# The second attention of a two-layer kernel: stages ordered engine by engine, router logits in groups of four tiles

## The reference

```python
h = _layernorm(x, axis=-1) * (1 + ca) + sa
x = x + ga * _L1_attn_ref(h, L1_attn_Wq, L1_attn_Wk, L1_attn_Wv, L1_attn_Wfc)
h = _layernorm(x, axis=-1) * (1 + cb) + sb
x = x + gb * _L1_ffn_ref(h, L1_ffn_Wg, L1_ffn_W1, L1_ffn_W2)
```

```python
Q = (x @ Wq.T).reshape(b, s, h, hd)
K = (x @ Wk.T).reshape(b, s, h, hd)
V = (x @ Wv.T).reshape(b, s, h, hd)
scores = jnp.einsum('bshd,bstd->bsht', Q, K) / math.sqrt(hd)
attn = jax.nn.softmax(scores, axis=-1)
out = jnp.einsum('bsht,bstd->bshd', attn, V).reshape(b, s, dm)
return out @ Wfc.T
```

## Time and profile before

| | us |
|---|---|
| median of 3 runs | 1048.62 |
| lowest and highest run | 1046.36, 1049.32 |
| span of the profiled execution | 1045.7 |
| TensorE busy in the span | 959.2 (92%) |
| VectorE busy | 690.6 (66%) |
| ScalarE busy | 496.8 (48%) |
| GpSimd busy | 377.1 (36%) |

### The profile page before, as it was taken

The page is one execution under the profiler, slowest core; times in us unless marked ns, Lnnn a source line. Parts: engine busy times, 40 slices in busy tenths (PEclk is TensorE's granted clock), DMA queues, the critical chain, the costliest instruction groups (busy, mean ns, idle before and its releaser), DMA issues. The chain is left out here.

```text
span 1045.7 us, 30362 instructions
## 1 busy us (share of the span) xinstructions
PE 959.2 (92%) x11177; PEld 823.6 (79%) x11178; DVE 690.6 (66%) x1747; ACT 496.8 (48%) x1343; POOL 377.1 (36%) x330
## 2 busy tenths in 40 slices
PE   6899999889999999999987999999767888999996
PEld 3466666879999999999965778888666878899995
DVE  3478877855777777777412688889985776344442
ACT  3556665404454554554446777777552440322221
POOL 0134335521223223222213455555561101455552
PEclk9999999999999999999998899999868999999998
DMA  9885581294232222221055657766421620444441
GB/s 338 216 331 122 126 269 41 97 386 115 85 102 79 87 97 85 89 92 71 8 107 92 115 124 150 154 134 128 99 68 57 266 108 22 151 134 140 134 136 35
DMA packets 133025, 135.59 MB, mean 130 GB/s; under 512 B 73884, under 2 KB 122142, under 8 KB 130740
## 3 DMA queue, kind: packets, MB, share of 16 engines
q1 hardware_dynamic: 121684, 90.80, 31.5%
q0 software_dynamic: 11232, 43.27, 13.0%
HBM read 96.21 MB, written 44.77 MB: 135 GB/s over the span
## 5 line engine op out<-in xcount | busy, mean ns | idle before, releaser
L1151 PE MATMUL psall<-rows 128*128 128x128 f32 x1872 | 224.8, 277 | 1.6 <-issue 1.1
L1151 PEld LDWEIGHTS psall<-rows 128*128 128x128 f32 x1872 | 219.6, 194 | 3.1 <-issue 1.3
L1114 POOL DMA_INDIRECT x<-ffn_rows,tok_i x78 | 82.6, 1059 | 171.8 <-DVE tok_i L999 69.9
L1165 PE MATMUL psall<-whi,rows 128*128 x624 | 141.0, 379 | 0.0
L1244 DVE COPY rows<-wlo 128x2048 f32 (+2 forms) x78 | 74.5, 955 | 95.8 <-PE psall L1151 85.2
L1165 PEld LDWEIGHTS psall<-whi,rows 128*128 128x128 f32 x624 | 115.7, 190 | 14.1
L1119 POOL DMA_INDIRECT attn_rows<-rows,tok_i x39 | 41.7, 1070 | 183.9 <-DVE rows L1276 183.9
L1504 DVE STREAM_TRANSPOSE whi<-whi 32x512 f32<-32x512 f32 x128 | 89.7, 701 | 9.1 <-POOL whi L1467 7.7
L1584 ACT ACTIVATE whi<-psall 32x512 f32<-32x512 f32 x128 | 75.3, 588 | 30.8 <-PE psall L1713 27.3
L280 PE MATMUL psall<-cst 128*128 128x128 f32 x714 | 88.4, 280 | 0.5 <-PEq L1387 0.5
L1306 ACT ACTIVATE rows<-psall,vs 128x128 f32<-128x128 f32 x312 | 85.0, 383 | 4.4 <-PE psall L1151 2.1
(11 more groups left out here) (250 smaller groups left out, 1731.3 us busy)
## 6 DMA issues: line engine op xcount, KB each, us to landing
ffn_rows<-mod_rows SPq DMA_DIRECT2D x2, 4096.0 KB
wlo<-in_W SPq DMA_DIRECT2D x2, 4096.0 KB, 17.5
whi<-in_w SPq DMA_DIRECT2D x5, 1024.0 KB
whi<-mod_rows SPq DMA_DIRECT2D x4, 1024.0 KB, 15.0
ffn_rows<-rows SPq DMA_DIRECT2D x8, 512.0 KB
ffn_rows<-x SPq DMA_DIRECT2D x8, 512.0 KB
wlo<-attn_rows SPq DMA_DIRECT2D x32, 128.0 KB, 3.4
v_turn<-wlo SPq DMA_DIRECT2D x32, 128.0 KB, 2.6
```

Source lines behind the costliest of these rows:

```text
L1114: eng.indirect_dma_start(xin[j % DEEP], None, src_d, bass.IndirectOffsetOnAxis(tok_i[:, j:j + 1].bitcast(U32), 0), bounds_check=T, oob_is_ ...
L1151: last = eng.matmul(b_up[t.par][f // 4][:, (f % 4) * P:(f % 4 + 1) * P], w_now[:, c, f * P:(f + 1) * P], inT[t.par][:, c * P:(c + 1) * P], ...
L1165: last = eng.matmul(b_dn[t.par][:, 0:D], hidT[t.par][:, f * P:(f + 1) * P], w_down[:, bass.ds(e, 1), f, :].rearrange("p o n -> p (o n)"), ...
```

## The change

`tile_steps` no longer uses common lags. Every stage has a lag of its own for its engine, every engine's list has a new order, in normal steps and in those with a projection, and the loop stops six steps early (`DRAIN`); what is left is written out call by call on each engine. Waits for shared banks follow counters (`put`) kept while the queue is written instead of `done_by`, so that `turn_n`, `turn_h` and the two logits stages each wait until all that was put into bank 6 before has been copied out. Router logits of all tiles but the last four are made for four tiles at once, as in attention 0, with a transpose; `h1T` needs four buffers instead of six. `gate_attention` signals after each of its four products. On SyncE the lags of `load_x` and `layer_rows` go from 14 to 16 and from 16 to 18, `load_v` from 7 to 8, `turn_k` from 6 to 5; `load_x` waits for all stores issued so far. No `hold_clock` is left behind the first scores.

```diff
-        LAG_N, LAG_V, LAG_VST, LAG_QK, LAG_VLD, LAG_S = 2, 3, 4, 6, 7, 10
-        LAG_MX, LAG_EX, LAG_ET, LAG_PV, LAG_Y = 11, 12, 13, 14, 15
-        LAG_XLD, LAG_ROW, LAG_X, LAG_H = 14, 16, 19, 20
+        LAG_N, LAG_SHIFT, LAG_V, LAG_KEEP_V, LAG_QK, LAG_KEEP_QK, LAG_Y, LAG_TURN_H = 1, 2, 3, 3, 5, 6, 15, 20
+        LAG_PV, LAG_LG, LAG_TURN_LG, LAG_S, LAG_COMP, LAG_COMP_REST, LAG_EX, LAG_OT = 14, 20, 20, 11, 11, 11, 13, 15
+        LAG_H1T, LAG_KEEP_LG, LAG_KEEP_TURNED, LAG_RSTD, LAG_H, LAG_SUM, LAG_MX, LAG_GATE = 20, 21, 21, 19, 19, 12, 11, 15
+        LAG_STAT, LAG_ET, LAG_MASK, LAG_NORM, LAG_SUB, LAG_X, LAG_NLD, LAG_VST = 18, 12, 10, 11, 11, 17, 0, 4
+        LAG_VLD, LAG_KT, LAG_XLD, LAG_ROW, LAG_ST = 8, 5, 16, 18, 20
+        DRAIN = 6
...
-            for s in range(NT + LAG_Y):
+            for s in range(NT + LAG_Y - DRAIN):
...
-                        eng.wait_ge(s_fin, 16 * (2 + 2 * B + done_by(t, LAG_XLD, LAG_H, 1)))
+                        assert len(stored) >= TB * (b - 2)
+                        eng.wait_ge(s_fin, 16 * (2 + 2 * B + len(stored)))
...
-                tile_steps([(0, load_norm), (LAG_VST, store_v), (LAG_VLD, load_v), (LAG_XLD, load_x), (LAG_ROW, layer_rows),
-                            (LAG_H, store_rows), (LAG_QK, turn_k)])
...
+                tile_steps([(LAG_VST, store_v), (LAG_ST, store_rows), (LAG_ROW, layer_rows), (LAG_NLD, load_norm),
+                            (LAG_VLD, load_v), (LAG_KT, turn_k), (LAG_XLD, load_x)],
...
-                    eng.wait_ge(c_["ya"], b + 1)
+                    eng.wait_ge(c_["ya"], t + 1)
...
-                tile_steps([(LAG_ET, normalize_exp), (LAG_X, add_attention), (LAG_MX, mask_other), (LAG_MX, sub_max)])
...
+                tile_steps([(LAG_SUB, sub_max), (LAG_X, add_attention), (LAG_MASK, mask_other),
+                            (LAG_NORM, normalize_exp)],
+                           [(LAG_X, add_attention), (LAG_SUB, sub_max), (LAG_MASK, mask_other),
+                            (LAG_NORM, normalize_exp)])
+                mask_other(31); sub_max(30); sub_max(31); add_attention(24); normalize_exp(30); add_attention(25)
...
-                            last = eng.tensor_tensor(yb[:, k, :], b_y[k], mod3[b % 2][:, 0, :], ALU.mult)
-                        last.then_inc(c_["ya"], 1)
+                            eng.tensor_tensor(yb[:, k, :], b_y[k], mod3[b % 2][:, 0, :], ALU.mult).then_inc(c_["ya"], 1)
...
-                tile_steps([(LAG_H, norm2), (LAG_ET, turn_exp), (LAG_X, stats_sum), (LAG_MX, max_scores), (LAG_EX, sum_exp),
-                            (LAG_Y, gate_attention)])
...
+                tile_steps([(LAG_GATE, gate_attention), (LAG_H, norm2), (LAG_SUM, sum_exp), (LAG_MX, max_scores),
+                            (LAG_STAT, stats_sum), (LAG_ET, turn_exp)],
+                           [(LAG_H, norm2), (LAG_GATE, gate_attention), (LAG_SUM, sum_exp), (LAG_STAT, stats_sum),
+                            (LAG_MX, max_scores), (LAG_ET, turn_exp)])
+                sum_exp(29); stats_sum(23); max_scores(30); norm2(22); norm2(23); turn_exp(29); max_scores(31); sum_exp(30)
+                gate_attention(27); sum_exp(31); stats_sum(24); turn_exp(30); stats_sum(25); norm2(24); turn_exp(31)
+                norm2(25); stats_sum(26); stats_sum(27); norm2(26); norm2(27); gate_attention(31); stats_sum(28)
+                stats_sum(29); stats_sum(30); norm2(28); stats_sum(31); norm2(29); norm2(30); norm2(31)
...
+                def keep_turned_logits(t):
+                    if t % TB == TB - 1:
+                        eng.wait_ge(c_["lg"], 2 * (t // TB) + 1)
+                        for k in range(TB):
+                            last = eng.activation(affT[QD * k:QD * k + E, :], b_lgT[QD * k:QD * k + E, :], ACT.Copy)
+                        last.then_inc(c_["key"], 1)
...
-                tile_steps([(LAG_MX, compact((0, 1), False)), (LAG_N, shift_h), (LAG_V, keep_v), (LAG_EX, exps), (LAG_MX, compact((2, 3), True)),
-                            (LAG_H, keep_h1T), (LAG_QK, keep_qk), (LAG_PV, keep_oT), (LAG_H, keep_logits), (LAG_X, rstd2)],
...
+                tile_steps([(LAG_KEEP_LG, keep_turned_logits), (LAG_EX, exps), (LAG_KEEP_TURNED, keep_group_logits),
+                            (LAG_OT, keep_oT), (LAG_KEEP_QK, keep_qk), (LAG_SHIFT, shift_h),
+                            (LAG_COMP, compact_first), (LAG_KEEP_V, keep_v), (LAG_H1T, keep_h1T),
+                            (LAG_COMP_REST, compact_rest), (LAG_RSTD, rstd2)],
...
+                def rows_bank_read():
+
+                    wait_some(eng, c_["hT"], put["turn_n"])
+                    wait_some(eng, c_["h1T"], put["turn_h"])
+                    wait_some(eng, c_["key"], put["logits"])
...
-                    wait_some(eng, c_["oT"], done_by(t, LAG_V, LAG_PV, 1))
+                    wait_some(eng, c_["oT"], put["weigh"])
...
+                def group_logits(t):
+                    if t % TB == TB - 1:
+                        eng.wait_ge(c_["h1T"], t + 1)
+                        rows_bank_read()
+                        put["logits"] += 1
+                        for c in range(C):
+                            for k in range(TB):
+                                last = eng.matmul(b_lgT[QD * k:QD * k + E, :], wg[:, c, :], h1T[k][:, c * P:(c + 1) * P], start=c == 0, stop=c == C - 1)
+                        last.then_inc(c_["lg"], 1)
+
+                def turn_logits(t):
+                    if t % TB == TB - 1:
+                        rows_bank_read()
+                        put["logits"] += 1
+                        eng.transpose(b_lgB, affT, ident).then_inc(c_["lg"], 1)
...
-                tile_steps([(LAG_N, turn_n), (LAG_V, values), (LAG_QK, queries_keys), (LAG_H, turn_h), (LAG_PV, hold_last), (LAG_PV, weigh),
-                            (LAG_H, logits), (LAG_S, scores)],
...
+                tile_steps([(LAG_S, scores), (LAG_V, values), (LAG_TURN_H, turn_h), (LAG_QK, queries_keys),
+                            (LAG_LG, group_logits), (LAG_PV, weigh), (LAG_TURN_LG, turn_logits), (LAG_N, turn_n)],
+                           [(LAG_S, scores), (LAG_V, values), (LAG_TURN_LG, turn_logits), (LAG_QK, queries_keys),
+                            (LAG_Y, project), (LAG_TURN_H, turn_h), (LAG_PV, weigh), (LAG_N, turn_n),
+                            (LAG_LG, group_logits)])
+                scores(30); turn_h(21); scores(31); weigh(27); weigh(28); project(27); turn_h(22); turn_h(23); group_logits(23)
+                turn_logits(23); weigh(29); turn_h(24); weigh(30); weigh(31); turn_h(25); project(31); turn_h(26)
+                turn_h(27); group_logits(27); turn_logits(27); turn_h(28); logits(28); turn_h(29); turn_h(30); logits(29)
+                turn_h(31); logits(30); logits(31)
```

More of the change, by code:

```diff
@@ L1340, in two_layer_kernel @@
         vrow = [cw(D) for _ in range(2)]
-        h1T = [cw(D) for _ in range(2 + TB)]
+        h1T = [cw(D) for _ in range(TB)]
         mod3 = [cw(3 * D).rearrange("p (j d) -> p j d", d=D) for _ in range(2)]
@@ L1371, in tile_steps @@
                         stage(s - lag)
-        def done_by(t, lag, other, steps_ago=0):
-            return min(max(t + lag - other - steps_ago + 1, 0), NT)
         names = "nT hT v ve qk qke ss comp msk mx sub ex sm mul et pv oT y ya xa mv2 rs2 h tH h1T lg key"
@@ new lines, in _ @@
+                exps(28); compact_first(30); compact_rest(30); keep_oT(26); keep_h1T(21); exps(29); keep_oT(27); rstd2(22)
+                rstd2(23); compact_first(31); compact_rest(31); exps(30); exps(31); keep_oT(28); keep_h1T(22); keep_h1T(23)
+                keep_turned_logits(23); rstd2(24); keep_oT(29); keep_group_logits(23); keep_h1T(24); rstd2(25); keep_oT(30)
+                keep_oT(31); rstd2(26); rstd2(27); keep_h1T(25); keep_h1T(26); keep_h1T(27); keep_turned_logits(27)
+                rstd2(28); rstd2(29); rstd2(30); keep_h1T(28); keep_group_logits(27); rstd2(31); keep_h1T(29); keep_h1T(30)
@@ L1624, in _ @@
+                keep_h1T(31); keep_logits(28); keep_logits(29); keep_logits(30); keep_logits(31)
             @block.tensor
@@ L1630, in _ @@
                 eng.wait_ge(s_wa, 16 + 16 * (2 + TB))
+                put = dict.fromkeys(("turn_n", "turn_h", "values", "weigh", "scores", "project", "logits"), 0)
+                def rows_bank_read():
+                    wait_some(eng, c_["hT"], put["turn_n"])
+                    wait_some(eng, c_["h1T"], put["turn_h"])
+                    wait_some(eng, c_["key"], put["logits"])
                 def turn_n(t):
                     eng.wait_ge(s_n1[t % 4], 16 * (t // 4 + 1))
-                    wait_some(eng, c_["hT"], t)
-                    wait_some(eng, c_["key"], done_by(t, LAG_N, LAG_H, 1))
+                    rows_bank_read()
+                    put["turn_n"] += 1
                     for c in range(C):
@@ L1643, in values @@
                     wait_some(eng, c_["ve"], t)
-                    wait_some(eng, c_["oT"], done_by(t, LAG_V, LAG_PV, 1))
```

(37 more changed lines are left out.)

60 lines of the change are left out of this document (28 added, 32 removed).

## The result

The changed kernel takes 1067.79 us (median; 1066.68 to 1068.69), against 1048.34 us for the kernel before, run beside it (1046.36 to 1049.32). The ratio is 1.0197, 95% interval 1.0178 to 1.0217: **19.4 us slower**, where 24.7 us less was forecast. The profiled span is 1064.8 us against 1045.7. Attention 1 takes 312.6 us from its first turn to its last logits, before 295.9, so 16.7 of the 19.1 us lie in it.

What follows compares the result with a forecast made beforehand. It took TensorE to bound the middle, VectorE close behind, and the tile-to-tile chain to decide filling and drain. 5 + 5.2 + 2 + 2.5 + 9 + 2 - 1 = 24.7 us off 1048.62 gave 1024 us, range 1012 to 1036.

Steps and rivals of the forecast that it cites:

- part 8: SyncE's queue: load_x comes two steps later, with 10 us for a load of 5.9 us; cost nothing.
- add_attention waiting for a DMA: Sign of being wrong, at the gate on GpSimd: load_x would land too late, against a forecast cost of nothing.
- Part 1: Logits four tiles at a time on TensorE: net 1.4 us less a batch, in seven of eight groups.
- I take 0.1: Stall a batch, in us, from turn_n waiting behind turn_logits and its copy in bank 6; range nothing to 0.5.
- Part 2: norm2 moved away from GpSimd's normalize_exp: VectorE gains 1.2 us a batch (0 to 2.4), hidden in the middle, counting in the drain.
- rival A: norm2 meets GpSimd's mask_other and keeps its 1.73 us: 7 us lost in all, 1031 us; chance 0.18.
- Part 3: Four TensorE-bound middle batches of the second attention: 1.3 us gained in each, 5.2 us in all.
- Part 4: Head and filling, up to the first projection: turn_n and queries_keys start a step earlier; 5 us gained (0 to 9).
- Part 5: Drain until the last projection: gains of 2, 2.5 and 9 us in its three batches.
- Part 6: After the last projection, until the last logits are copied: 2 us gained (0 to 3).
- Part 7: 57 filler matmuls that kept TensorE's clock up are removed: 1 us lost (0 to 4.5).
- rival C: The drain is not shortened, as the written-out order meets another wait: 1035 us; chance 0.12.

Runs made afterwards that it cites:

- Experiments 1 to 3: layer_rows moved on SyncE: changed kernel at lag 16, 1032.73 us; changed kernel at lag 18 but first in the step, 1037.05 us; kernel before at lag 18, 1079.3 us.
- e1_row16: The changed kernel with layer_rows back from lag 18 to lag 16 on SyncE; 1032.73 us, ratio 0.9838 to the kernel before.
- experiment 4: e1_row16 with the logits of tiles 0 to 27 made tile by tile again; 1047.82 us, ratio 0.9991 to the kernel before.
- experiment 6: e1_row16 with norm2 behind sum_exp on VectorE again, as in the kernel before; 1044.98 us, ratio 0.9968 to the kernel before.
- experiment 8: e1_row16 with 36 filler matmuls on the identity between TensorE's written-out last calls; 1035.98 us, ratio 0.9892 to the kernel before.
- e9_before_adjoining: The kernel before with turn_h ahead of queries_keys on TensorE, so queries_keys and weigh stand side by side; 1063.35 us, ratio 1.0148.
- e10_turn_h_between: e1_row16 with turn_h between queries_keys and weigh in normal steps, and the group's logits behind weigh; 1048.21 us, ratio 0.9989 to the kernel before.

## Why the prediction was wrong, point by point

**The step that failed is part 8, SyncE's queue.** It priced the load that moves from lag 14 to 16 (`load_x`), found its cover and wrote "Cost nothing". That was right for `load_x`: add_attention never waits for it. But the same line of the diff moves `layer_rows` from 16 to 18, and the prediction never asked who needs its rows. The arithmetic was at hand. The projection of batch b is at step 4b + 3 + 15 = 4b + 18. `layer_rows` acts on tile 4b, so lag 16 puts it at 4b + 16, two steps ahead of the gate, and lag 18 in the gate's own step, in SyncE's list behind two stores (`store_v`, `store_rows`) and two loads (`load_v`, `load_norm`). None of the rivals had this either. "add_attention waiting for a DMA" stood among the signs of being wrong, one instruction away from the true one. Experiments 1 to 3 show the cause from both sides: 35 us back, most of it by place in the queue, and 31 us lost by it in the old kernel.

The sum closes within 1 us. The six batches behind the first projection take 211.9 us in the changed kernel and 177.1 in `e1_row16`: 34.8. TensorE's waits for the gate are 30.4; six stretches at the lower clock, estimated at 1.9 each, are 11.4; and the changed kernel has 6.2 us fewer stops in them (2.9 against 9.1). 30.4 + 11.4 - 6.2 = 35.6. Batch by batch the same sum is off by 0.8 to 2.6 us either way, most in the sixth, where `e1_row16` is at a low clock too (0.70), so that it closes so well is in part luck. The filling took 4.4 us back in that pair of profiles, but it varies from 68.4 to 72.8 us among the kernels here with the same TensorE order.

The other parts can be read in `e1_row16`, whose attention takes 282.1 us, 13.8 less than before, against the 24.7 forecast.

- **Part 1 (group logits).** Durations right: 0.62 us for the group and 0.30 for the turn. In the middle 1.4 us a batch is what experiment 4 finds. The rest of its 15 us lies mostly in the last batches, 5.7 of it in two projections at the lower clock, and the prediction had no term for that. "I take 0.1" for bank 6 was mis-sized: 1.06 us a batch; I left the second wait, turn_logits for its own copies, out.
- **Part 2 (norm2).** VectorE's busy time in four batches falls from 104.98 to 100.74 us, 1.06 a batch; 1.2 was taken. The two products take 1.16 us together, where about 1 was given as the sign. The worth of the place was underrated: 12 us in experiment 6, more than the 7 of rival A, and 6.5 of them in the four middle batches, where turn_h too waits for norm2.
- **Part 3 (the middle).** 5.2 us forecast, 3.4 us lost: four batches take 121.1 us, before 117.7. TensorE works 3.0 us less (113.86 to 110.87), as forecast in kind (5.6 by part 1), and the wait for the gate, 3.2 us before, is nearly gone (0.2). Against that stand 6.8 us of idle time in stops and 3.1 us of bank 6. No row of the middle of the kernel before could show the stops, since it had none there.
- **Part 4 (filling).** 5 forecast; the first projection comes 6.5 us earlier in the changed kernel, 2.1 in `e1_row16`.
- **Part 5 (drain).** Right. The fifth and sixth batch lose 4.1 us (4.5 forecast), the last one 10.3 (9 forecast).
- **Part 6.** 2 forecast, 0.7 found.
- **Part 7.** 1 us lost by the missing fillers was forecast; experiment 8 shows that putting some in, at other places, costs 3 to 6 us.

2.1 - 3.4 + 4.1 + 10.3 + 0.7 = 13.8. With the rows in time, rival C's figure (1035) would have been near, though for the opposite reason: the drain was shortened, the middle was not.

## What to carry to other kernels

When a diff changes a table of lags, take each lag by itself: write down the step in which its result is needed, the step in which it is now issued and what stands ahead of it in that queue, for the small loads too. A transfer that nobody ever waited for leaves no row among the waits, so its slack has to be worked out from its issue, its landing and the step that uses it. And a hole of a few microseconds in the queue of the bounding engine, here TensorE, can cost more than its length: by the estimate above a third again, through the clock.

## What the hardware showed that was not expected

- TensorE stops inside a group of matmuls that waits for nothing that the profile names: 0.3 to 1.7 us, 11 times in `e1_row16`, where 64 + 64 small matmuls adjoin, and 3.03 us once in `e9_before_adjoining`; never in the order of before. The cause is open.
- After a wait of 5.93 us the scores take 2.09 us in place of 1.17, and values 2.08. The granted clock is 0.50 behind each of the five waits of 4.7 to 6.0 us. The Trainium skill (TensorE: Matmul & The Clock Gate, HAM oscillation — how this bites in real kernels) warns of idle gaps between bursts of matmuls; these five agree. Shorter holes do it at times: behind waits of 2.00 and 0.57 us in `e10_turn_h_between` a queries_keys takes 3.23 us in place of 1.95, but behind the stop of 1.66 us in `e1_row16` the clock is 1.00.
- Three 128 KB loads of rows, 3.2 us from issue to landing in the median, were enough to hold three engines in six of the eight batches. In the one shown VectorE is held for 8.45 us, TensorE for 5.93 and GpSimd for 11.87: the gate waits for the rows, and the scores and the sums with the residual wait for the gate.
